# Four VectorE sums at a kernel's end made two, and the stores of banks 5 and 7 joined

## The chip, the core and the metric

The kernel runs on one core of a Trainium2 chip. The metric is device time in microseconds (us), the median of several executions. Time before: 98.53 us, the median of three runs (97.7 to 98.61).

## What is computed

The input x is 8 images of 64 channels and 32 x 32 pixels, in float32. Two blocks follow one another. The first is a linear attention with 8 heads of 32 on the layer-normalised input, with its projection, bias and residual. The second is a 3 x 3 convolution of the sign of the input with the signs of the weights, then a batch norm over all images and pixels, and the residual. Only the second block's end matters here:

```python
def _L1_conv_ref(x, W, gamma, beta):
    s = jnp.sign(x)
    bw = jnp.sign(W)
    y = lax.conv_general_dilated(s, bw, window_strides=(1, 1), padding=((1, 1), (1, 1)), ...)
    mean = jnp.mean(y, axis=(0, 2, 3))
    var = jnp.var(y, axis=(0, 2, 3))
    inv = gamma / jnp.sqrt(var + BN_EPS)
    yn = (y - mean[None, :, None, None]) * inv[None, :, None, None] + beta[None, :, None, None]
    return yn + x
```

The output is 8 x 64 x 32 x 32 in float32, 2 MB in all.

## The kernel before, in words

Two images lie side by side on the 128 partitions: image 2q on partitions 0 to 63 and image 2q+1 on 64 to 127, for the four pairs q. An image has 1024 pixels, two halves of 512. The instructions of each engine are written out by hand in one list per engine, and semaphores order the engines among one another: `t_ready` counts what ScalarE has scaled, `o_ready` what VectorE has summed, `x1_moved` the transfers that bring parts of x into place, `stored` and `stored_pool` the stores.

The convolution leaves its 8 x 512 columns in the eight banks of PSUM (`ps`), one bank per 128 x 512 block. Banks 0 and 1 hold the two halves of images 0 and 1 (pair 0) with the images on their usual partitions. Banks 2 and 3 hold pair 1 with the partitions of the two images exchanged, so image 3 is on partitions 0 to 63 and image 2 on 64 to 127. Bank 4 has the first half of pair 2 and bank 6 that of pair 3, straight; banks 5 and 7 hold the second halves of these pairs, exchanged. The residual x must match: for banks 0, 1, 4 and 6 it is read from `X`, for 2, 3, 5 and 7 from `X1`, which SyncE's transfers of L282 and L286 fill with the partitions exchanged.

TensorE's last convolutions are those of pairs 2 and 3 (L1002). Then a short serial part makes the batch norm's scale and shift (`bn`), of columns of one element (L710 to L775). After it comes the end of the kernel, which the change touches. It works in nine pieces in the order of `FINALS` (L46): bank 4 in two halves of 256 columns, then banks 6, 0, 1, 5, 7, 2, 3.

- ScalarE (L559) writes scale x y of one piece into `OUT`, one ACTIVATE per piece. Bank 0 it reads from `Y`, a float16 copy of that bank in SBUF.
- VectorE (L781) adds shift and residual to it in place, one SCALAR_TENSOR_TENSOR per piece.
- SyncE stores. It issues a store of 128 KB for each half of bank 4, one of 256 KB for bank 6 (L291), one of 512 KB for banks 0 and 1 together after the sum of bank 1 (L293), then the stores of partitions 0 to 63 of banks 5, 7 (L296), 2 and 3 (L299), 128 KB each.
- GpSimd (POOL) issues the stores of partitions 64 to 127 of banks 5, 7 (L391), 2 and 3 (L394), 128 KB each. Its descriptors are made in software; the profile has these stores on the queue q0, and SyncE's on q1.

SyncE's last wait is for all twelve stores (8 and 4). ScalarE's order of pieces is not touched by the change.

```python
for i, piece in enumerate(FINALS):
    dve.wait_ge(t_ready, i + 1)
    wait_residual(dve, piece)
    nc.vector.scalar_tensor_tensor(cut(OUT, piece), cut(OUT, piece), bn[:, BN_SHIFT], residual(piece),
                                   op0=ALU.add, op1=ALU.add).then_inc(o_ready, 1)
```

Of the kernel before, what the change touches and what calls it, by code (L numbers as in the profile page):

```python
# [5 lines left out]
def attention_then_binary_conv(nc, x, ln_g, ln_b, w_qkv, w_out, b_out, conv_w, bn_gamma, bn_beta, out):  # L6
# [11 lines left out]
    B, C, H, W = x.shape  # L18
    P = 128
    N = H * W  # L20
# [5 lines left out]
    PAIRS = B // 2  # L26
    BANK = 512
# [15 lines left out]

    HALF = BANK // 2
    PIECES = {"4a": (4, 0, HALF), "4b": (4, HALF, BANK), **{str(j): (j, 0, BANK) for j in range(8)}}
    FINALS = ("4a", "4b", "6", "0", "1", "5", "7", "2", "3")  # L46
    ACT_STATS = (2, 3)
    RECORDS = 4
# [3 lines left out]
    out_d = out.rearrange("b c h w -> b c (h w)")  # L52
# [4 lines left out]
    with ExitStack() as ctx:  # L57
        def sb(name, shape, dt=f32):
            return ctx.enter_context(nc.sbuf_tensor(name, shape, dt))

        def sem(name):
            return ctx.enter_context(nc.semaphore(name))
# [34 lines left out]
        X = sb("X", [P, PAIRS, N])  # L97
# [23 lines left out]
        X1 = sb("X1", [P, B, BANK])  # L121
        OUT = sb("OUT", [P, B, BANK])
# [5 lines left out]
        bn = sb("bn", [P, 5])  # L128
        BN_SPREAD, BN_LN, BN_INV, BN_SCALE, BN_SHIFT = (slice(i, i + 1) for i in range(5))
# [65 lines left out]
        t_ready, o_ready, stored, stored_pool = sem("t_ready"), sem("o_ready"), sem("stored"), sem("stored_pool")  # L195
# [5 lines left out]
                engine.wait_ge(hi_ready, n - 1)  # L201

        def wait_final(engine, piece):
            engine.wait_ge(o_ready, FINALS.index(piece) + 1)

        def cut(t, piece):
            j, first, end = PIECES[piece]
            return t[:, j, first:end]

        def residual(piece):  # L210
            j, first, end = PIECES[piece]
            if j < 2:
                return X[:, 0, j * BANK + first:j * BANK + end]
            return X[:, j // 2, first:end] if j in (4, 6) else X1[:, j, first:end]

        def wait_residual(engine, piece):
            j = PIECES[piece][0]
            if j < 2 or j in (4, 6):
                engine.wait_ge(x1_ready, HALVES * (j // 2) + (2 if j < 2 else 1))
            else:  # L220
                engine.wait_ge(x1_moved[j // 2], 32)
# [20 lines left out]
        def _(sp):  # L242
# [15 lines left out]
            for h in range(HALVES):  # L258
                part = slice(h * BANK, (h + 1) * BANK)
# [28 lines left out]
            for piece in ("4a", "4b", "6"):  # L288
                j, first, end = PIECES[piece]
                wait_final(sp, piece)  # L290
                sp.dma_start(out_p[j // 2, :, first:end], OUT[:, j, first:end]).then_inc(stored, 16)  # L291
            wait_final(sp, "1")
            sp.dma_start(out_p[0], OUT[:, 0:2, :]).then_inc(stored, 16)  # L293
            for q in range(2, PAIRS):
                wait_final(sp, str(2 * q + 1))
                sp.dma_start(out_d[2 * q + 1, :, BANK:N], OUT[0:C, 2 * q + 1, :]).then_inc(stored, 16)  # L296
            for h in range(HALVES):
                wait_final(sp, str(2 + h))
                sp.dma_start(out_d[3, :, h * BANK:(h + 1) * BANK], OUT[0:C, 2 + h, :]).then_inc(stored, 16)  # L299
            sp.wait_ge(stored, 16 * 8)  # L300
            sp.wait_ge(stored_pool, 16 * 4)

        @block.gpsimd
        def _(pool):
# [81 lines left out]
                    nc.gpsimd.tensor_tensor(e_lo, e, e_hi, ALU.subtract).then_inc(elo_pool, 1)  # L386

            nc.gpsimd.memset(act_records[:, :, 0:1], float(len(ACT_STATS) * BANK // RECORDS)).then_inc(st_counts, 1)
            for q in range(2, PAIRS):
                wait_final(pool, str(2 * q + 1))  # L390
                pool.dma_start(out_d[2 * q, :, BANK:N], OUT[C:P, 2 * q + 1, :]).then_inc(stored_pool, 16)  # L391
            for h in range(HALVES):
                wait_final(pool, str(2 + h))
                pool.dma_start(out_d[2, :, h * BANK:(h + 1) * BANK], OUT[C:P, 2 + h, :]).then_inc(stored_pool, 16)  # L394
# [2 lines left out]
        def _(act):  # L397
# [159 lines left out]
            act.wait_ge(scale_ready, 1)  # L557
            for piece in FINALS:
                nc.scalar.activation(cut(OUT, piece), cut(ps, piece) if piece != "0" else Y[:], ACT.Identity,  # L559
# [3 lines left out]
        def _(dve):  # L563
# [211 lines left out]
            nc.vector.scalar_tensor_tensor(bn[:, BN_SHIFT], fs_ps[:, 0:1], bn[:, BN_SCALE], vec[:, OUT_:OUT_ + 1],  # L775
                                           op0=ALU.mult, op1=ALU.add).then_inc(affine_ready, 1)
            dve.wait_ge(affine_ready, 1)
            for i, piece in enumerate(FINALS):
                dve.wait_ge(t_ready, i + 1)
                wait_residual(dve, piece)  # L780
                nc.vector.scalar_tensor_tensor(cut(OUT, piece), cut(OUT, piece), bn[:, BN_SHIFT], residual(piece),  # L781
                                               op0=ALU.add, op1=ALU.add).then_inc(o_ready, 1)

        @block.tensor
# [407 lines left out]
```

## Time and profile before

| | |
|---|---|
| median of three runs | 98.53 us |
| the profiled execution | 98.15 us |
| its span in the trace | 96.4 us |
| TensorE (PE) busy in the span | 80.3 us |
| VectorE (DVE) busy | 62.0 us |
| ScalarE (ACT) busy | 57.0 us |
| GpSimd (POOL) busy | 43.6 us |
| bytes written to HBM | 2.10 MB |

The profile describes one execution. Its own time is 1.75 us longer than the span, which runs from the first to the last recorded event. Positions in the trace are us from the span's start. Busy shares over the whole span say little about the end of the kernel, where TensorE has nothing left to do, so this document reads the last ten microseconds by themselves.

### The profile page before, as it was taken

To read this page: it belongs to the slowest core of one execution; us is meant where nothing else is said; L and a number is where in the kernel's file an instruction comes from. 1 tells how busy PE (TensorE), PEld (TensorE's weight loads), DVE (VectorE), ACT (ScalarE), POOL (GpSimd) and SP (SyncE) were. 2 spreads that over 40 slices of the span, in tenths; PEclk is the share of its full clock that TensorE was granted. 3 is DMA by queue.
4 is the path that set the end of the run, shared out by engine and by line. 5 is a ranking of instruction groups with operands and counts; after the bars stand their busy time and mean duration, and the time that the engine had idled before them with its cause. 6 is when DMAs were issued, how large, how long until landed. Compare 5 with 4: busy or idle time off the path is not lost.

```text
span 96.4 us, 2071 instructions
## 1 busy us (share of the span) xinstructions
PE 80.3 (83%) x763; PEld 46.4 (48%) x763; DVE 62.0 (64%) x125; ACT 57.0 (59%) x113; POOL 43.6 (45%) x58
## 2 busy tenths in 40 slices
PE   4999988999999899999999999999999999410000
PEld 4624433357576357565756747767664544210000
DVE  5723587985499708836965499719935359639920
ACT  5024967788799559079492753777601479069700
POOL 6912789469671594162495093586400000000440
PEclk9999999999999999999999999999999999995555
DMA  2799013314300123000033000001700404003795
GB/s 70 225 290 363 5 37 97 111 39 136 106 8 0 51 63 107 7 0 0 0 108 113 0 0 0 0 7 24 194 7 0 109 7 100 9 0 127 298 259 190
DMA packets 4613, 7.87 MB, mean 82 GB/s; under 512 B 1410, under 2 KB 1982, under 8 KB 4604
## 3 DMA queue, kind: packets, MB, share of 16 engines
q1 hardware_dynamic: 4140, 7.16, 23.5%
q0 software_dynamic: 192, 0.52, 1.8%
q8 instruction: 6, 0.10, 0.5%
q10 hardware_dynamic: 272, 0.07, 0.3%
q14 instruction: 3, 0.02, 0.1%
HBM read 2.51 MB, written 2.10 MB: 48 GB/s over the span
## 4 chain that ended last, share of the span: by engine, by line
PE 71%; DVE 13%; ACT 6%; issue 4%; POOL 2%; POOLq 1%; DVEq 0%
PE ps L899 9%; PE ps L913 8%; PE ps L900 7%; PE ps L990 5%; PE ps L1002 4%; PE ps L925 4%; PE ps L793 4%; PE ps L970 4%; PE ps L862 4%; DVE mx L629 4%; PE ps L945 3%; DVE OUT L781 2%; PE ps L952 2%; PE ps L931 2%; PE ps L1042 2%
## 5 line engine op out<-in xcount | busy, mean ns | idle before, releaser
L634 DVE TENSOR_REDUCE mxp<-ps 128x2 bf16<-128x1024 f32 x12 | 14.7, 1223 | 10.9 <-PE ps L862 10.8
L476 ACT ACTIVATE E<-ps 128x512 f32<-128x512 f32 x32 | 17.8, 596 | 3.4 <-PE ps L900 3.2
L386 POOL TENSOR_TENSOR E_lo<-E 128x512 bf16<-128x512 f32 x11 | 12.5, 1161 | 7.1 <-ACT E L476 7.1
L899 PE MATMUL ps<-wk_max,S 128*128 128x256 bf16 x64 | 15.2, 275 | 0.0
L900 PE MATMUL ps<-wk_lo,S 128*128 128x256 bf16 x64 | 15.1, 272 | 0.0
L391 POOL DMA_DIRECT2D out<-OUT x2 | 1.2, 605 | 22.0 <-DVE OUT L781 22.0
L405 ACT ACTIVATE sq<-ps 128x512 f32<-128x512 f32 x8 | 4.8, 601 | 8.3 <-DVE bn_eps L599 3.7
L342 POOL TENSOR_TENSOR x_lo<-XN,x_hi 128x512 bf16<-128x512 f32 x8 | 9.2, 1156 | 0.9 <-DVE x_hi L610 0.8
L702 DVE SCALAR_TENSOR_TENSOR X<-XN,vec,ps 128x1024 f32<-128x1024 f32 (+1 forms) x5 | 5.2, 1066 | 5.4 <-PE ps L970 5.4
L899 PEld LDWEIGHTS ps<-wk_max,S 128*128 128x128 bf16 x64 | 6.2, 97 | 4.3 <-issue 1.5
L331 POOL CAST x_hi<-XN 128x512 bf16<-128x512 f32 x6 | 3.7, 611 | 9.4 <-DVE XN L604 9.4
L913 PE MATMUL ps<-E,XT 128*64 128x256 f32 x64 | 7.8, 385 | 0.0
L483 ACT COPY PT<-ps 128x256 f32<-128x256 f32 x8 | 3.0, 372 | 7.5 <-PE ps L931 5.6
L409 ACT ACTIVATE lnv<-ps,eps 128x512 f32<-128x512 f32 x8 | 5.5, 683 | 2.7 <-PE ps L814 2.7
L900 PEld LDWEIGHTS ps<-wk_lo,S 128*128 128x128 bf16 x64 | 6.3, 98 | 1.2 <-issue 0.3
L604 DVE TENSOR_TENSOR XN<-ps,rstd 128x512 f32<-128x512 f32 x8 | 5.5, 685 | 1.9 <-ACT rstd L415 1.7
L316 POOL TENSOR_TENSOR x_rest<-X 128x512 f32<-128x512 f32 x4 | 4.2, 1040 | 3.9 <-DMA X<-in_x 3.9
L487 ACT ACTIVATE SG<-X,vec 128x1024 bf16<-128x1024 f32 (+1 forms) x5 | 4.8, 980 | 1.9 <-DVE X L702 1.9
L781 DVE SCALAR_TENSOR_TENSOR OUT<-OUT,bn,X 128x512 f32<-128x512 f32 (+1 forms) x9 | 5.6, 689 | 0.3 <-ACT OUT L559 0.3
L793 PE MATMUL ps<-X,center_mat 128*128 128x512 f32 x8 | 5.7, 856 | 0.1
L629 DVE TENSOR_REDUCE mx<-ps 128x1 bf16<-128x1024 f32 x4 | 4.9, 1223 | 1.2 <-PE ps L851 1.1
L913 PEld LDWEIGHTS ps<-E,XT 128*64 128x64 f32 x64 | 4.2, 136 | 2.5 <-issue 0.7
(148 smaller groups left out, 167.0 us busy)
## 6 DMA issues: line engine op xcount, KB each, us to landing
X<-in_x SPq DMA_DIRECT2D x3, 512.0 KB, 4.5
S<-x_hi SPq DMA_DIRECT2D x7, 126.0 KB
S<-x_lo SPq DMA_DIRECT2D x7, 126.0 KB
out<-OUT SPq DMA_DIRECT2D x6, 128.0 KB, 2.9
X<-in_x SPq DMA_DIRECT2D x2, 256.0 KB, 3.0
X<-X SPq DMA_DIRECT2D x2, 256.0 KB, 3.4
X<-X SPq DMA_DIRECT2D x4, 128.0 KB, 2.3
out<-OUT SPq DMA_DIRECT2D x1, 512.0 KB, 2.7
```

The source lines that it names most:

```text
L342: nc.gpsimd.tensor_tensor(x_lo[:, q, part], XN[:, q, part], x_hi[:, q, part], ALU.subtract).then_inc(lo_ready, 1)
L386: nc.gpsimd.tensor_tensor(e_lo, e, e_hi, ALU.subtract).then_inc(elo_pool, 1)
L409: nc.scalar.activation(lnv[:, n % 2, :], pv(n), ACT.Ln, bias=eps[:, 0:1]).then_inc(lnv_ready, 1)
L476: nc.scalar.activation(E[:, b % 2, 2 * g:2 * g + 2, :].rearrange("p k j -> p (k j)"), kt_ps[g % 2], ACT.Exp).then_inc(exp_ready, 1)
L604: nc.vector.tensor_tensor(XN[:, q, h * BANK:(h + 1) * BANK], pc(n), rstd[:, n % 2, :], ALU.mult).then_inc(scaled, 1)
L629: nc.vector.tensor_reduce(mx[:, d, t:t + 1], k_ps.rearrange("p a n -> p (a n)"), AX.X, ALU.max).then_inc(max_ready, 1)
L634: nc.vector.tensor_reduce(mxp[:, h, :, t], k_ps, AX.X, ALU.max).then_inc(max_ready, 1)
L781: nc.vector.scalar_tensor_tensor(cut(OUT, piece), cut(OUT, piece), bn[:, BN_SHIFT], residual(piece), op0=ALU.add, op1=ALU.add).then_inc(o_ ...
L793: nc.tensor.matmul(pc(n), center_mat[:], x_unit, start=True, stop=True).then_inc(centered, 1)
L899: nc.tensor.matmul(dst, chunk, wk_max[:, b % 2, :], start=True, stop=False)
L900: last = nc.tensor.matmul(dst, chunk, wk_lo[:], start=False, stop=True)
L913: last = nc.tensor.matmul(d_ps[d * C:d * C + C, :], XT[:, b, k, :], E[:, b % 2, k, :], start=(k < 2), stop=(k >= CH - 2))
```

## The change

VectorE makes seven sums instead of nine: the list `SUMS` says what each covers. The sum of bank 0 and that of bank 1 become one operation on 128 x 1024, and those of banks 5 and 7 one operation on 128 x 2 x 512 (banks 5 and 7 of `OUT` and `X1`, with bank 6 stepped over). Each waits until ScalarE has scaled its last member. ScalarE still scales bank by bank. SyncE's store of banks 0 and 1 waits for the merged sum, as one of 512 KB like before. SyncE's two stores of banks 5 and 7 become one of 256 KB, and so do GpSimd's two.

```diff
@@ -43,6 +43,7 @@
+    SUMS = ("4a", "4b", "6", "0+1", "5+7", "2", "3")
     FINALS = ("4a", "4b", "6", "0", "1", "5", "7", "2", "3")
@@ -201,7 +202,7 @@
         def wait_final(engine, piece):
-            engine.wait_ge(o_ready, FINALS.index(piece) + 1)
+            engine.wait_ge(o_ready, SUMS.index(piece) + 1)
@@ -289,16 +290,15 @@
-            wait_final(sp, "1")
+            wait_final(sp, "0+1")
             sp.dma_start(out_p[0], OUT[:, 0:2, :]).then_inc(stored, 16)
-            for q in range(2, PAIRS):
-                wait_final(sp, str(2 * q + 1))
-                sp.dma_start(out_d[2 * q + 1, :, BANK:N], OUT[0:C, 2 * q + 1, :]).then_inc(stored, 16)
+            wait_final(sp, "5+7")
+            sp.dma_start(out_d[5:8:2, :, BANK:N].rearrange("j c n -> c j n"), OUT[0:C, 5:8:2, :]).then_inc(stored, 16)
...
-            sp.wait_ge(stored, 16 * 8)
-            sp.wait_ge(stored_pool, 16 * 4)
+            sp.wait_ge(stored, 16 * 7)
+            sp.wait_ge(stored_pool, 16 * 3)
@@ -386,9 +386,9 @@
-            for q in range(2, PAIRS):
-                wait_final(pool, str(2 * q + 1))
-                pool.dma_start(out_d[2 * q, :, BANK:N], OUT[C:P, 2 * q + 1, :]).then_inc(stored_pool, 16)
+            wait_final(pool, "5+7")
+            pool.dma_start(out_d[4:8:2, :, BANK:N].rearrange("j c n -> c j n"), OUT[C:P, 5:8:2, :]
+                           ).then_inc(stored_pool, 16)
@@ -775,10 +775,19 @@
-            for i, piece in enumerate(FINALS):
-                dve.wait_ge(t_ready, i + 1)
-                wait_residual(dve, piece)
-                nc.vector.scalar_tensor_tensor(cut(OUT, piece), cut(OUT, piece), bn[:, BN_SHIFT], residual(piece),
+            for piece in SUMS:
+                members = piece.split("+")
+                dve.wait_ge(t_ready, FINALS.index(members[-1]) + 1)
+                for member in members:
+                    wait_residual(dve, member)
+                if piece == "0+1":
+                    part = OUT[:, 0:2, :].rearrange("p j n -> p (j n)")
+                    kept = X[:, 0, :]
+                elif piece == "5+7":
+                    part, kept = OUT[:, 5:8:2, :], X1[:, 5:8:2, :]
+                else:
+                    part, kept = cut(OUT, piece), residual(piece)
+                nc.vector.scalar_tensor_tensor(part, part, bn[:, BN_SHIFT], kept,
                                                op0=ALU.add, op1=ALU.add).then_inc(o_ready, 1)
```

VectorE's last instructions before, with the semaphores that each waits for (the first two rows are the halves of bank 4; the next covers banks 6, 0 and 1; then 5, 7, and 2 with 3):

```order
L781 SCALAR_TENSOR_TENSOR OUT<-OUT,bn,X 128x256 [waits x1_ready,t_ready,affine_ready]
L781 SCALAR_TENSOR_TENSOR OUT<-OUT,bn,X 128x256 [waits x1_ready,t_ready]
L781 SCALAR_TENSOR_TENSOR OUT<-OUT,bn,X 128x512 [waits x1_ready,t_ready] x3
L781 SCALAR_TENSOR_TENSOR OUT<-OUT,bn,X 128x512 [waits x1_moved2,t_ready]
L781 SCALAR_TENSOR_TENSOR OUT<-OUT,bn,X 128x512 [waits x1_moved3,t_ready]
L781 SCALAR_TENSOR_TENSOR OUT<-OUT,bn,X 128x512 [waits x1_moved1,t_ready] x2
```

And in the changed kernel:

```order
L790 SCALAR_TENSOR_TENSOR OUT<-OUT,bn,X 128x256 [waits x1_ready,t_ready,affine_ready]
L790 SCALAR_TENSOR_TENSOR OUT<-OUT,bn,X 128x256 [waits x1_ready,t_ready]
L790 SCALAR_TENSOR_TENSOR OUT<-OUT,bn,X 128x512 [waits x1_ready,t_ready]
L790 SCALAR_TENSOR_TENSOR OUT<-OUT,bn,X 128x1024 [waits x1_ready,t_ready]
L790 SCALAR_TENSOR_TENSOR OUT<-OUT,bn,X 128x2x512 [waits x1_moved3,x1_moved2,t_ready]
L790 SCALAR_TENSOR_TENSOR OUT<-OUT,bn,X 128x512 [waits x1_moved1,t_ready] x2
```

Banks 0 and 1 now stand in one row of 1024 columns, banks 5 and 7 in one of 2 x 512, which waits for the transfers of both pairs. Nothing else on VectorE has moved.

SyncE's last instructions before (L291 stores banks 4 and 6, L293 banks 0 and 1, L296 banks 5 and 7, L299 banks 2 and 3; L57 is the end of its list):

```order
L291 DMA out<-OUT 128x256 [waits o_ready] x2
L291 DMA out<-OUT 128x512 [waits o_ready]
L293 DMA out<-OUT 128x1024 [waits o_ready]
L296 DMA out<-OUT 64x512 [waits o_ready] x2
L299 DMA out<-OUT 64x512 [waits o_ready] x2
L57 UNCONDITIONAL_BRANCH [waits stored_pool,stored]
```

And in the changed kernel:

```order
L292 DMA out<-OUT 128x256 [waits o_ready] x2
L292 DMA out<-OUT 128x512 [waits o_ready]
L294 DMA out<-OUT 128x1024 [waits o_ready]
L296 DMA out<-OUT 64x2x512 [waits o_ready]
L299 DMA out<-OUT 64x512 [waits o_ready] x2
L58 UNCONDITIONAL_BRANCH [waits stored_pool,stored]
```

One store of 64 x 2 x 512 stands where two of 64 x 512 stood, and GpSimd's list changes in the same way.

## Rows read from the trace of the kernel before

**Rows 1.** Busy time by stretch; columns PE, PEld, DVE, ACT, POOL, clock, DMA share, GB/s

```profile
82.50:86.50 4.00, 0.90 (x8) 0.59 (x4) 2.05 (x5) 1.27 (x5) 0.00 (x0) 1.00 0.00 0
86.50:92.20 5.70, 0.00 (x0) 0.00 (x0) 5.61 (x9) 4.37 (x8) 1.64 (x3) 0.51 0.58 207
92.20:96.40 4.20, 0.00 (x0) 0.00 (x0) 0.00 (x0) 0.00 (x0) 0.60 (x2) 0.50 0.68 220
```

**Rows 2.** End of the chain that ended last: start us, us, what

```profile
89.40 0.76 DVE OUT L781
90.16 0.30 issue
90.45 1.21 POOL out L391 x2
...
92.55 0.54 POOLq L57
```

**Rows 3.** Timeline: pieces of ScalarE (banks 6, 1, 7, 3), VectorE (6, 0, 1, 3)

```profile
86.68 0.69 ACT L559 ACTIVATE OUT<-ps,bn 128x512 f32<-128x512 f32 x1
...
87.86 0.69 ACT L559 ACTIVATE OUT<-ps,bn 128x512 f32<-128x512 f32 x1
...
89.00 0.71 ACT L559 ACTIVATE OUT<-ps,bn 128x512 f32<-128x512 f32 x1
...
90.14 0.73 ACT L559 ACTIVATE OUT<-ps,bn 128x512 f32<-128x512 f32 x1
...
87.40 0.75 DVE L781 SCALAR_TENSOR_TENSOR OUT<-OUT,bn,X 128x512 f32<-128x512 f32 x1
...
88.07 0.75 DVE L781 SCALAR_TENSOR_TENSOR OUT<-OUT,bn,X 128x512 f32<-128x512 f32 x1
...
88.73 0.75 DVE L781 SCALAR_TENSOR_TENSOR OUT<-OUT,bn,X 128x512 f32<-128x512 f32 x1
...
91.39 0.75 DVE L781 SCALAR_TENSOR_TENSOR OUT<-OUT,bn,X 128x512 f32<-128x512 f32 x1
```

**Rows 4.** Groups by line, shapes apart: busy us, mean ns of one, idle us before

```profile
L781 DVE SCALAR_TENSOR_TENSOR OUT<-OUT,bn,X 128x512 f32<-128x512 f32 x7 | 4.7, 748 | 0.0
L702 DVE SCALAR_TENSOR_TENSOR X<-XN,vec,ps 128x1024 f32<-128x1024 f32 x3 | 3.8, 1280 | 4.0 <-PE ps L970 4.0
...
L702 DVE SCALAR_TENSOR_TENSOR X<-XN,vec,ps 128x512 f32<-128x512 f32 x2 | 1.4, 745 | 1.4 <-PE ps L970 1.4
```

**Rows 5.** Timeline: issues of stores by SyncE and GpSimd

```profile
89.51 0.33 SPq L293 DMA_DIRECT2D out<-OUT  x1
...
90.45 0.68 POOL L391 DMA_DIRECT2D out<-OUT  x1 [21.96 <-DVE OUT L781]
...
92.58 0.52 POOL L394 DMA_DIRECT2D out<-OUT  x1 [0.29 <-issue]
```

**Rows 6.** DMA queues, 91.5 to 92.0 and 92.0 to 92.5: packets, MB, share

```profile
q1 hardware_dynamic: 68, 0.12, 89.7%
...
q0 software_dynamic: 12, 0.05, 37.9%
```

**Rows 7.** Busy time by stretch of 0.5 us, columns as in rows 1

```profile
90.00:90.50 0.50, 0.00 (x0) 0.00 (x0) 0.50 (x2) 0.50 (x2) 0.05 (x1) 0.50 0.34 139
90.50:91.00 0.50, 0.00 (x0) 0.00 (x0) 0.50 (x2) 0.37 (x1) 0.50 (x1) 0.50 1.02 418
...
92.00:92.50 0.50, 0.00 (x0) 0.00 (x0) 0.13 (x1) 0.00 (x0) 0.28 (x1) 0.50 0.82 197
...
94.50:95.00 0.50, 0.00 (x0) 0.00 (x0) 0.00 (x0) 0.00 (x0) 0.00 (x0) 0.50 0.98 357
95.00:95.50 0.50, 0.00 (x0) 0.00 (x0) 0.00 (x0) 0.00 (x0) 0.00 (x0) 0.50 0.31 119
```

**Rows 8.** Stores of L291 (128 and 256 KB), then of L394 (128 KB)

```profile
DMA to landing us min/median/max: 1.9/1.9/2.0
...
DMA to landing us min/median/max: 3.3/3.4/3.5
```

## The prediction, made before the changed kernel ran

> **What bounds the kernel now.** I read four views in this order. First, the busy time of each engine by stretch [rows 1]: up to 86.5 us TensorE and the short serial batch-norm part set the pace, and the change touches nothing there. From 86.5 to 92.2 VectorE is busy for 5.61 of 5.70 us, and from 92.2 to the end of the span no compute engine works, while the DMA engines are at 68%. So the end has two halves: sums paced by VectorE, then stores that drain. Second, the chain that ended last [rows 2]: it runs through a sum of VectorE, then through GpSimd's store issues, the last near 92.6, and then to the end at 96.4. Third, the timeline of the pieces [rows 3] and of the store issues [rows 5]. Fourth, the DMA engines in steps of half a microsecond [rows 6, 7], because the chain doesn't say whether the last 3.8 us are the latency of one store or a backlog of several.
>
> They are a backlog. The first three stores (128, 128 and 256 KB) land 1.9 to 2.0 us after issue, with idle DMA engines before them, and GpSimd's last two, of 128 KB, take 3.3 to 3.5 us [rows 8]. That is 1.4 us of queueing. The DMA engines show it directly: from 90.5 to 95.0 the share is between 0.82 and 1.10 in each of the nine half microseconds (three of them stand in [rows 7]), and 0.31 in the last stretch with data. Data of the 512 KB store of banks 0 and 1 start to flow near 90.3 (a third of the full rate in the half microsecond from 90.0 [rows 7], 0.8 us behind the issue at 89.51 [rows 5]) and the last data at about 95.3 (a share of 0.31 in the stretch from 95.0). Thus 1.5 MB (banks 0, 1, 5, 7, 2, 3) flow in some 5 us, and after them about 1.1 us pass for completion. What sets the end is when this backlog starts, how fast it flows, and whether it runs dry.
>
> **VectorE, step by step.** Two sums of 512 columns follow each other at 88.73 - 88.07 = 0.66 us from start to start, although each lasts 0.75 [rows 3]: their ends overlap by 0.09. For 1024 columns the same operation takes 1.28 us [rows 4], on operands partly in PSUM; at 512 columns that form took 745 ns in this trace against 748 here, so I use 1.28 for both merged sums. With the same overlap the next sum starts 1.28 - 0.09 = 1.19 after it, against 2 x 0.66 = 1.33 for two. Each merge saves 0.14 us, both 0.28. I charge nothing for stepping over bank 6; bounds are zero and the cost of an unmerged pair, 0.14.
>
> Against that stands a wait. Before, the sum of bank 0 starts at 88.07. The merged one must wait for ScalarE's bank 1, which starts at 87.86 and lasts 0.69, so it ends at 88.55 [rows 3]. With 0.05 for the hand-over (bank 6 was scaled at 86.68 + 0.69 = 87.37 and its sum began at 87.40; bounds 0.02 and 0.10) the merged sum starts at 88.60: VectorE idles for 0.53 us, with all later sums queued behind it. It ends at 88.60 + 1.28 = 89.88, where the sum of bank 1 ended at 88.73 + 0.75 = 89.48. The sum of 5+7 can start at 88.60 + 1.19 = 89.79. ScalarE is ahead there: it scales bank 7 from 89.00 to 89.71 and the last piece from 90.14 to 90.87 [rows 3]. The wait for bank 7 is covered, by less than 0.1 us; if ScalarE is 0.1 later it costs up to that. The sum 5+7 ends at 89.79 + 1.28 = 91.07, bank 2 starts at 90.98 and bank 3 at 91.65, ending at 92.40, where it ended at 91.39 + 0.75 = 92.14 [rows 3]. The last sum is 0.53 - 0.28 = 0.26 us later.
>
> **The stores, step by step.** SyncE issues the store of 0+1 within 0.03 us of its sum, at 89.91 instead of 89.51: 0.40 later. The stores of bank 5 (sum from 89.40 to 90.15 before [rows 2]) are issued 0.92 later, those of bank 7 (90.81 before) 0.26 later, those of bank 2 and 3 also 0.26. So no store leaves earlier, and two instructions on SyncE and GpSimd are gone. Behind GpSimd's 5+7 stand its stores of 2 and 3, and only the end of the kernel waits for them.
>
> How far can the backlog absorb this? Its front moves from 90.3 to 90.7. The 512 KB at 418 GB/s [rows 7] last 1.25 us, to about 91.95. SyncE's 5+7 is issued at 91.10 and its data can flow 0.8 later, at 91.9: no gap. Then 256 KB more of it, 0.6 to 1.0 us by the 418 GB/s or the slower 250 seen when mostly SyncE's 2 KB rows of banks 5 and 7 flowed (0.12 MB in 91.5 to 92.0) [rows 6], so until 92.5 to 92.9. GpSimd's data come late: its first store was issued at 90.45 [rows 5] and q0 has no packet before the stretch from 92.0 [rows 6], 1.6 us later. With 0.30 for its hand-over [rows 2], the merged store is issued at 91.37 and flows from about 93.0. SyncE's bank 2 (issued 91.77, data from 92.6) fills the hole between. So I expect the DMA engines busy throughout, with a gap of at most 0.4 us.
>
> The backlog therefore ends later by about its later front, 0.40 us, less what fewer and larger stores give back, plus a gap if there is one. The bounds: it gives back at most the whole 1.4 us of queueing, less 0.26 of the later issue, so -1.1 us; it loses at most 0.40 for the front and 0.4 for a gap and some 0.35 for GpSimd (below), +1.15. I take +0.35, near the later front and a little under it, since the last issue is only 0.26 later.
>
> **GpSimd's merged issue** is a price that the trace doesn't show. For 64 x 512 it takes 0.52 to 0.68 us [rows 5]; for 64 x 2 x 512 it is between 0.52 and twice 0.6 = 1.2. At 0.6 it is done at 91.97, before bank 2 is summed (91.73 + 0.30 = 92.03), and costs nothing. At 1.2 it is done at 92.57, bank 2 goes out 92.57 to 93.09, and bank 3 at 93.1, instead of 92.58 before: 0.5 late, of which the queueing hides part. I take 0.9, halfway: done at 92.27, bank 2 until 92.79, bank 3 at 92.84, 0.26 late, which is the delay of VectorE anyway.
> The Trainium skill (DMA: Bandwidth & Descriptors, section Anatomy of one DMA) calls the generation of descriptors a small and variable part and says that many can be emitted before the extra cost shows. By that the merged issue would stay at about 0.6, the same sum as mine; no row before has a larger store of GpSimd to set beside it.
>
> The sum: 98.15 us of the profiled execution (span 96.4 and 1.75 around it) + 0.35 = 98.5. That execution lies 0.38 under the median of the three runs, 98.53; the middle of all four times is 98.34, so I forecast 98.34 + 0.35 = 98.7 us.
>
> **The rivals.**
> 1. The stores flow better. In the stretch from 92.0 the share is 0.82 and only 197 GB/s flow, and 357 GB/s in that from 94.5 [rows 7], so the engines seem held up while the 2 KB rows of 5 and 7 from both queues mix. If the merged stores, which overlap less, flow like the late stretch, the 0.22 MB between 91.5 and 92.5 need 0.63 instead of 1.0 us and those to 93.5 likewise about 0.2 less. That gives 0.55 back against 0.40: -0.15, 98.2 us. For it speaks the uneven rate; against it, that the same rows, the same 64 partitions and the same two queues remain.
> In the Trainium skill (DMA: Bandwidth & Descriptors, section Bandwidth) the rule is to batch transfers, towards 1 MiB, and the section on one DMA gives each a fixed 2.0 us. Its formula makes 2.3 us of a 128 KB store where the trace has 3.3 to 3.5, so by it 1.1 us are queueing; two stores fewer would be worth something only where their fixed parts lie one behind the other.
> Here a merged chain that removed all queueing of [rows 8] would give the -1.1 us above, 97.2 us. The issues stand 0.5 to 0.8 us apart while each store takes over 3, so the fixed parts overlap already; this has little chance.
> 2. VectorE alone decides and the stores follow the last issue: +0.26 and nothing more, 98.6 us. This differs from my forecast by the front of the backlog, and can hardly be told from it by time.
> 3. Slower by over 1%: the queue runs dry and GpSimd is late. The store of 5+7 leaves 0.92 us later than bank 5 did. If GpSimd's issue takes 1.2 us and its first data come later in proportion, near 93.6, the DMA engines drain SyncE's share by 93.0 and idle until then, and over 0.5 MB then flow behind it on q0. That is 0.40 of the front, 0.4 of a gap and 0.35 of GpSimd's last issue: +1.15, 99.5 us. It decides once the first packet of q0 comes after about 93.3. For it speaks the long 1.6 us from GpSimd's issue to data; against it, that 1.4 us of queueing are there to absorb a late last store.
> 4. The merged sums cost as much as two (1.5 us each), or the stepped one does: +0.14 to +0.28 on top of mine, 98.9 us. The row of 1.28 us for 1024 columns speaks against it.
>
> **How the numbers follow.** My case 0.47; rival 1 in its mild form 0.20, with a gain of over 1 us 0.03; rival 2 0.13; rival 3 0.10; rival 4 0.07. About 1% is what a measurement of this kernel can tell from no change, near 1 us. Forecast, rivals 1 (mild), 2 and 4 lie within it, though their upper tails reach over; so faster 0.06, same 0.82, slower 0.12. The range goes from 97.9, below the mild rival 1 by a spread like that of the runs (0.3), to 99.5, the whole of rival 3: it leaves out the large gain and the outer spread of either side.
>
> **What would show each step.** The merged sum of 0 and 1 starts near 88.6 after an idle time of about 0.5 us that ScalarE ended, and lasts 1.28; the last sum starts near 91.65. The issue of the 512 KB store stands at 89.9, the last issue of GpSimd near 92.8. The DMA share stays near 1 from 90.8 to 95.3 and data end near 95.7. I would be wrong if the DMA engines run empty between 92 and 93.5 (rival 3), if the last stores land in less than 3 us although they are issued later (rival 1), or if GpSimd's merged issue takes over 1.1 us.

## The result, and the profile after

The changed kernel takes 99.09 us in the median (98.84 to 99.69, 4 runs), the kernel before 98.12 us in the same comparison (97.11 to 98.61, 4 runs). The ratio is 1.0138, with a 95% interval of 1.0088 to 1.0189: the change makes the kernel 1.4% slower. The ratio leaves out runs over 1.5% above the fastest of their kernel, here the one of 98.61 us, and so is larger than the quotient of the medians (1.0099). The forecast was 98.7 us. The range of 97.9 to 99.5 holds the result, but the likeliest case was "within 1%", and the measured ratio lies above that. What holds it is the upper end, which came from rival 3 and not from the case that was forecast.

The profiled execution took 99.19 us, with a span of 97.4 us against 96.4. Its busy time by stretch answers to the last two of [rows 1]. Columns are PE, PEld, DVE, ACT, POOL, granted clock, DMA share, GB/s:

```profile
86.50:92.20 5.70, 0.00 (x0) 0.00 (x0) 5.19 (x7) 4.11 (x8) 1.08 (x2) 0.50 0.48 184
92.20:97.40 5.20, 0.00 (x0) 0.00 (x0) 0.00 (x0) 0.00 (x0) 0.72 (x2) 0.50 0.78 203
```

VectorE works less (5.19 for 5.61 us), the DMA engines carry less beside it (share 0.48 for 0.58), and the stretch in which no compute engine works is 5.2 us instead of 4.2. The loss shows there.

One more thing is needed to set traces side by side. Everything up to the first piece that ScalarE scales is untouched, yet it begins at other times in other executions: at 85.95 us in the kernel before, at 85.69 here, between 85.0 and 86.5 in the runs below. So I call **the tail** the time from that start to the end of the span: 96.4 - 85.95 = 10.45 us before, 97.4 - 85.69 = 11.71 after. The tail is 1.26 us longer. Where the two are compared, 0.26 is to be added to a time of after. Every tail is that of one execution, with the span read to 0.1 us.

The timeline of the pieces and of the store issues answers to [rows 3, 5]:

```profile
87.61 0.69 ACT L559 ACTIVATE OUT<-ps,bn 128x512 f32<-128x512 f32 x1
...
88.33 1.28 DVE L790 SCALAR_TENSOR_TENSOR OUT<-OUT,bn,X 128x1024 f32<-128x1024 f32 x1 [0.44 <-ACT OUT L559]
...
89.64 0.33 SPq L294 DMA_DIRECT2D out<-OUT  x1
89.53 1.28 DVE L790 SCALAR_TENSOR_TENSOR OUT<-OUT,bn,X 128x1024 f32<-128x1024 f32 x1
...
90.84 0.71 SPq L296 DMA_DIRECT2D out<-OUT  x1
91.12 0.76 POOL L390 DMA_DIRECT2D out<-OUT  x1 [22.89 <-DVE OUT L790]
...
91.39 0.75 DVE L790 SCALAR_TENSOR_TENSOR OUT<-OUT,bn,X 128x512 f32<-128x512 f32 x1
...
92.24 1.82 SPq L299 DMA_DIRECT2D out<-OUT  x1
92.43 0.52 POOL L394 DMA_DIRECT2D out<-OUT  x1
```

VectorE does what was worked out, nearly to the hundredth. The sum of banks 0 and 1 waits 0.44 us for ScalarE and starts 88.33 - 85.69 = 2.64 us after the scaling began (forecast 88.60 - 85.95 = 2.65). The store of banks 0 and 1 goes out after 3.95 us (forecast 3.96). The last sum ends at 92.14, after 6.45 us (forecast 6.45; 6.19 before). So VectorE's part, 0.40 us at the front and 0.26 at the last sum, is as forecast, and the rest of the loss is elsewhere.

The DMA engines in half microseconds answer to [rows 7]:

```profile
91.00:91.50 0.50, 0.00 (x0) 0.00 (x0) 0.50 (x2) 0.00 (x0) 0.38 (x1) 0.50 0.95 393
91.50:92.00 0.50, 0.00 (x0) 0.00 (x0) 0.50 (x1) 0.00 (x0) 0.50 (x2) 0.50 0.51 205
92.00:92.50 0.50, 0.00 (x0) 0.00 (x0) 0.14 (x1) 0.00 (x0) 0.47 (x2) 0.50 0.54 123
92.50:93.00 0.50, 0.00 (x0) 0.00 (x0) 0.00 (x0) 0.00 (x0) 0.46 (x1) 0.50 0.94 197
93.00:93.50 0.50, 0.00 (x0) 0.00 (x0) 0.00 (x0) 0.00 (x0) 0.00 (x0) 0.50 0.97 172
...
95.50:96.00 0.50, 0.00 (x0) 0.00 (x0) 0.00 (x0) 0.00 (x0) 0.00 (x0) 0.50 0.93 201
96.00:96.50 0.50, 0.00 (x0) 0.00 (x0) 0.00 (x0) 0.00 (x0) 0.00 (x0) 0.50 0.67 238
```

Two things are new. From 91.5 to 92.5 the engines are half idle (0.51 and 0.54). And from 92.5 to 93.5 they are busy to 94% and 97%, but move only 172 to 197 GB/s, where they moved 393 from 91.0. The DMA queues of 93.0 to 93.5 and of 93.5 to 94.0 say whose data these are:

```profile
q1 hardware_dynamic: 42, 0.09, 97.2%
...
q0 software_dynamic: 32, 0.13, 88.2%
q1 hardware_dynamic: 24, 0.02, 19.1%
```

Until 93.5 SyncE's queue q1 is alone, with its store of 64 partitions. GpSimd's first packet starts at 93.56, 2.44 us behind the issue at 91.12; before it started at 92.19, 1.74 us behind the issue at 90.45 [rows 5]. The last stores pay for it. L299 (SyncE, banks 2 and 3) landed after 3.3 to 3.4 us before (the first line here), L394 (GpSimd) after 3.3 to 3.5 [rows 8]. The second line is L299 in the changed kernel, the third L394:

```profile
DMA to landing us min/median/max: 3.3/3.4/3.4
...
DMA to landing us min/median/max: 4.1/4.4/4.8
...
DMA to landing us min/median/max: 4.2/4.3/4.3
```

The last to land is SyncE's store of bank 3: issued at 92.24, plus 4.8, is 97.0. SyncE's issue of it lasts 1.82 us, where the corresponding one of before lasted 0.73. That long issue is over at 94.06, while the store of bank 2, ahead of it on q1, ends only between 94.6 and 95.3. So nothing here shows that the issue itself held the last data back.

### The profile page after: what moved, and what is told of

It is laid out like the page before. It is cut to its first block, busy times and chain, and to the rows that moved or that the text cites. A ratio compares the mean times of both kernels' runs of the same rounds, so it can differ in the third digit from the quotient of the medians.

```text
span 97.4 us, 2065 instructions
## 1 busy us (share of the span) xinstructions
PE 79.4 (82%) x763; PEld 46.2 (47%) x763; DVE 62.4 (64%) x123; ACT 57.0 (59%) x113; POOL 43.3 (44%) x57
## 4 chain that ended last, share of the span: by engine, by line
PE 67%; DVE 13%; ACT 6%; issue 3%; DMA 3%; POOL 2%; ACTq 0%; DVEq 0%
PE ps L908 8%; PE ps L922 8%; PE ps L909 7%; PE ps L999 5%; PE ps L1011 4%; PE ps L934 4%; PE ps L979 4%; PE ps L871 4%; DVE mx L629 4%; PE ps L802 3%; PE ps L954 3%; DMA X<-in_x 3%; DVE XN L604 2%; PE ps L961 2%; ACT OUT L559 2%
## 5 line engine op out<-in xcount | busy, mean ns | idle before, releaser
L790 DVE SCALAR_TENSOR_TENSOR OUT<-OUT,bn,X 128x512 f32<-128x512 f32 (+2 forms) x7 | 5.4, 824 | 0.8 <-ACT OUT L559 0.8
L802 PE MATMUL ps<-X,center_mat 128*128 128x512 f32 x8 | 5.1, 772 | 0.3 <-DMA X<-in_x 0.3
```

The lines of the kernel that those rows point to most:

```text
L790: nc.vector.scalar_tensor_tensor(part, part, bn[:, BN_SHIFT], kept, op0=ALU.add, op1=ALU.add).then_inc(o_ready, 1)
L802: nc.tensor.matmul(pc(n), center_mat[:], x_unit, start=True, stop=True).then_inc(centered, 1)
```

## The experiments

Each run is compared with the kernel before on the same chip. "Tail" is the time from the first scaled piece to the end of the span in the one profiled execution of each kernel.

| run | what is joined or changed | ratio to before | 95% interval | tail, us |
|---|---|---|---|---|
| before | nothing | | | 10.45 |
| the change | both sums, stores of 5 and 7 | 1.0138 | 1.0088 to 1.0189 | 11.71 |
| e1 | sum of 0 and 1 alone | 1.0066 | 1.0023 to 1.0109 | 10.92 |
| e2 | sum of 5 and 7, and their stores | 1.0145 | 1.0070 to 1.0220 | 11.66 |
| e3 | the stores alone | 1.0108 | 1.0063 to 1.0152 | 11.49 |
| e4 | both sums alone | 1.0116 | 1.0054 to 1.0178 | 11.44 |
| e5 | nothing; bank 5's stores wait for bank 7 | 1.0094 | 1.0058 to 1.0130 | 11.11 |
| e6 | SyncE's store alone | 1.0055 | 1.0015 to 1.0096 | 10.80 |
| e7 | GpSimd's store alone | 1.0034 | 0.9995 to 1.0072 | 10.80 |
| e8 | as e3, each store over 128 partitions | 1.0032 | 0.9997 to 1.0068 | 10.75 |
| e9 | as e3, other places in HBM | 1.0104 | 1.0055 to 1.0153 | 11.40 |
| p2 | as before, upper halves issued by ScalarE | 1.0032 | 0.9988 to 1.0077 | 10.32 |
| p3b | as before, two of them by ScalarE | 0.9979 | 0.9935 to 1.0022 | 10.39 |
| p4 | as before, half stores first | 1.0083 | 1.0043 to 1.0124 | 10.77 |

**e1: the sum of banks 0 and 1 alone.**

```diff
-    SUMS = ("4a", "4b", "6", "0+1", "5+7", "2", "3")
+    SUMS = ("4a", "4b", "6", "0+1", "5", "7", "2", "3")
```

with the stores of 5 and 7 apart as before. What was expected: 

> Only the sums of banks 0 and 1 are merged; 5 and 7 are summed and stored one by one as before. Theory M (the joined stores of banks 5 and 7 cost the most: a store over 64 partitions alone on the DMA engines moves some 190 GB/s, and GpSimd's data come late): +0.2 to +0.4 us against before, from VectorE's wait for bank 1, without an empty stretch of the DMA engines after 91.7 us and without a stretch of over 1 us in which q1 alone is busy. Rival W (VectorE's wait for bank 1, which delays every later store, is what costs): nearly the whole loss, +1.0 us or more.

Measured: +0.66%, about 0.65 us, and a tail longer by 0.47 us. The interval begins at +0.23%, so the loss is real and its size less sure. It is somewhat more than theory M's 0.2 to 0.4, far less than W's 1.0, and the tail fits the step of the prediction that put the front of the backlog 0.40 us later. The trace has none of the half-empty stretches (columns as above):

```profile
91.50:92.00 0.50, 0.00 (x0) 0.00 (x0) 0.50 (x1) 0.00 (x0) 0.40 (x2) 0.50 0.89 254
92.00:92.50 0.50, 0.00 (x0) 0.00 (x0) 0.15 (x1) 0.00 (x0) 0.31 (x1) 0.50 0.92 201
```

**e2: banks 5 and 7 alone**, sum and stores:

```diff
-    SUMS = ("4a", "4b", "6", "0+1", "5+7", "2", "3")
+    SUMS = ("4a", "4b", "6", "0", "1", "5+7", "2", "3")
```

What was expected: 

> Banks 0 and 1 are summed apart as before; 5 and 7 are summed in one and stored together. M: most of the loss, +0.8 to +1.2 us. VectorE waits about 0.3 us for ScalarE's bank 7 and its last sum ends some 0.2 us later. W: +0.2 us at most, since no wait for bank 1 is left.

Measured: +1.45%, a tail longer by 1.21 us. Without any wait for bank 1, the whole loss of the change is there. W is out as the main cause. VectorE is not quite as before, though: the merged sum waits 0.27 us for ScalarE's bank 7, and the last sum ends 0.21 us later (6.40 us after the first scaled piece, for 6.19). e3 takes that away.

**e3: the stores alone.** The nine sums are as before, `SUMS` is equal to `FINALS`, and both joined stores wait for the sum of bank 7:

```diff
-            wait_final(sp, "5+7")
+            wait_final(sp, "7")
```

What was expected: 

> VectorE's nine sums as before; only the stores of banks 5 and 7 are joined, both issued after the sum of bank 7. M: +0.6 to +1.0 us although no sum is late. W: 0 within 0.2 us.

Measured: +1.08%, a tail longer by 1.04 us, although no sum has moved and nothing was taken from or added to VectorE. Two DMA issues fewer, and a microsecond lost.

**e4: the sums alone**, both merged, and the stores of 5 and 7 apart but both behind the merged sum:

```diff
-            sp.dma_start(out_d[5:8:2, :, BANK:N].rearrange("j c n -> c j n"), OUT[0:C, 5:8:2, :]).then_inc(stored, 16)
+            for q in range(2, PAIRS):
+                wait_final(sp, "5+7")
+                sp.dma_start(out_d[2 * q + 1, :, BANK:N], OUT[0:C, 2 * q + 1, :]).then_inc(stored, 16)
```

What was expected: 

> Both pairs of sums are merged as in the change, but banks 5 and 7 are stored by two stores on either queue, issued one after the other behind the merged sum. M in the form that the joined transfer itself is slow: +0.3 to +0.5 us. M in the form that only the late start of bank 5's store counts (no half-finished data to overlap with banks 0 and 1): about the same as the change, +1.0 us or more. W: as the change too.

Measured: +1.16%, a tail longer by 0.99 us. So a loss of this size does not need a joined transfer, as the form with the late start had it. The merged sum of 0 and 1 is in this run too, and it alone makes the tail 0.47 us longer (e1), so e4 doesn't show that a late bank 5 is enough. e5 tests that.

**e5: the late start by itself.** Nine sums, four stores for banks 5 and 7, and only the wait of bank 5's stores changed to the sum of bank 7:

```diff
-                wait_final(sp, str(2 * q + 1))
+                wait_final(sp, "7")
```

and the same on GpSimd. What was expected: 

> Nine sums as before, and banks 5 and 7 stored apart as before, but the stores of bank 5 wait for the sum of bank 7 too. Theory L (the loss is the late start: data of bank 5 no longer follow banks 0 and 1 without a hole): +0.7 to +1.1 us against before, as with the joined stores alone (+1.08%). Theory J (joining makes the transfers slow, because q1's 256 KB run before anything of q0 and in one piece): +0.3 us or less, and packets of q1 near 84 ns once q0 is active.

Measured: +0.94%, a tail longer by 0.66 us. Theory L holds by the ratio, and the interval leaves out the 0.3 us of J: stores of bank 5 that wait 0.66 us longer, and whose bytes were not the last to leave, cost 0.9 us (0.66 by the tail). The gap of the DMA engines (share 0.48) and the slow stretch after it (189 GB/s) are both there, in the stretches from 92.0 and 92.5:

```profile
92.00:92.50 0.50, 0.00 (x0) 0.00 (x0) 0.37 (x1) 0.00 (x0) 0.50 (x2) 0.50 0.48 115
92.50:93.00 0.50, 0.00 (x0) 0.00 (x0) 0.00 (x0) 0.00 (x0) 0.50 (x2) 0.50 0.89 189
```

Whether joining adds something of its own is not settled. The tails say 0.38 us (1.04 against 0.66), the ratios 0.14% with intervals far wider than that. The packets give a reason for a difference of that kind: q1 flows alone from 92.16 to 93.52 in e3, 1.36 us, and from 92.25 to 92.88 in e5, 0.63 us.

**e6 and e7: one queue at a time.** Nine sums; in e6 only SyncE's store of 5 and 7 is joined, in e7 only GpSimd's. What was expected of e6: 

> Nine sums, only SyncE's stores of 5 and 7 are joined; GpSimd stores 5 and 7 one by one as early as before. L: about half of the loss, +0.3 to +0.6 us, the hole after 91.7 us is partly filled by q0 from 92.0. J with q1 at fault: +0.7 to +1.0 us.

And of e7: 

> Nine sums, only GpSimd's stores of 5 and 7 are joined; SyncE's are as before. The first packet of q0 moves from 92.1 to some 93.4 us. L: no hole after 91.7, q1 alone runs at about 200 GB/s until then: +0.4 to +0.7 us. J with q0 at fault: +0.8 us or more; J with q1 at fault: within 0.3 us of before.

Measured: +0.55% and +0.34%, with equal tails of 10.80 us (+0.35). The two together (e3) lose 1.08%. While one queue's bank 5 is on time its data fill the hole, so each alone costs about half of L's sum or less. For e7 that is under the 0.4 to 0.7 us that L had forecast, and near what J gave it with q1 at fault; e5 is what speaks against J. The stretch from 91.0 in e6 has GpSimd's data alone, in e7 SyncE's alone, one row of each:

```profile
91.00:91.50 0.50, 0.00 (x0) 0.00 (x0) 0.28 (x1) 0.00 (x0) 0.43 (x1) 0.50 1.13 238
...
91.00:91.50 0.50, 0.00 (x0) 0.00 (x0) 0.18 (x1) 0.00 (x0) 0.47 (x2) 0.50 0.81 209
```

Either queue alone with a store of 64 partitions moves 209 to 238 GB/s, GpSimd's over partitions 64 to 127, SyncE's over 0 to 63. That led to the question of the next two runs: why are these transfers slow?

**When GpSimd's data start.** e3 and e7 have the same joined store on GpSimd, and it is issued 5.16 us after the first scaled piece in both (91.07 - 85.91 and 90.16 - 85.00). Only SyncE's stores differ. In e3 q0's first packet starts at 93.52, 2.45 us behind the issue; in e7 at 91.80, 1.64 us behind it. So the larger store of GpSimd is not what makes its data late. The packets' own times in the traces say what goes with it: q0 starts when the SyncE store that was issued before it is ending. A store ends with 16 short packets. Those of that SyncE store start from 92.17 to 92.36 in the kernel before, and q0 at 92.19; from 93.55 to 93.80 in the changed one, and q0 at 93.56; from 91.85 to 92.02 in e8 below, and q0 at 92.05. In all thirteen kernels of this document in which GpSimd stores, q0's first packet lies between the start of the first of these packets and 0.04 us behind the end of the last. Two consecutive stretches of e8, from 91.5 and from 92.0, have q1 alone and then q0 alone:

```profile
q1 hardware_dynamic: 85, 0.14, 76.9%
...
q0 software_dynamic: 43, 0.18, 95.4%
q1 hardware_dynamic: 1, 0.00, 0.1%
```

**e8: the same stores over all partitions.** As e3, but SyncE stores bank 5 whole and GpSimd bank 7 whole. The exchange of the two images in the second halves of pairs 2 and 3 is left out.

```diff
-            sp.dma_start(out_d[5:8:2, :, BANK:N].rearrange("j c n -> c j n"), OUT[0:C, 5:8:2, :]).then_inc(stored, 16)
+            sp.dma_start(out_p[2, :, BANK:N], OUT[:, 5, :]).then_inc(stored, 16)
```

What was expected: 

> Nine sums and joined stores in number, bytes, row length and time of issue (after the sum of bank 7), but SyncE stores bank 5 over all 128 partitions and GpSimd bank 7 likewise. It leaves out the exchange of the two images of pairs 2 and 3 in their second halves. Theory P (a store over 64 partitions uses only half of SBUF's side, some 200 GB/s while it is alone): packets of 2 KB on q1 fall from 145 to 189 ns to near 84 ns, q1 alone moves over 350 GB/s, and the time falls by 0.5 us or more under the kernel with joined stores (+1.08%), to within 0.4 us of before. Rival H (the rows' places in HBM make them slow): packets stay over 140 ns and the time at +0.9 us or more.

Measured: +0.32% with an interval that reaches below zero, a tail of 10.75 us instead of 11.49. The intervals of e3 and e8 overlap only from 0.63% to 0.68%. The bytes, the row length, the number of stores and the point of issue are those of e3, and 0.7 us are back. The queue q1 of e8 from 91.5 to 92.0, with rows of 2 KB over 128 partitions, has the first line above; for e3 here is the same queue from 92.5 to 93.0, over 64:

```profile
q1 hardware_dynamic: 47, 0.10, 92.3%
```

The share is of 16 engines over 0.5 us, which is 8 us of engine time. In e3 0.923 x 8 = 7.4 us over 47 packets is 157 ns for a packet of 2 KB. In e8 0.769 x 8 = 6.15 us over 85 packets is 72 ns; 15 of these are the short ones that end a transfer, so it is near 88 ns for one of 2 KB. Over the whole half microsecond q1 moved 287 GB/s, not the 350 that P expected, since the engines were busy for 77% only. The rival H is not yet out by this, since e8 also changes which images the queues write.

The time that is back is not that of the rate alone. SyncE's issue of the store is shorter too, first e3, then e8:

```profile
90.79 0.71 SPq L296 DMA_DIRECT2D out<-OUT  x1
...
90.33 0.33 SPq L296 DMA_DIRECT2D out<-OUT  x1
```

Its data start 1.37 us behind the issue in e3 (at 92.16) and 0.84 us behind it in e8 (at 91.17). So the DMA engines are empty from 91.73 to 92.16 in e3 and not at all there in e8. e8 shows what half-partition stores cost here in rate and start together. It also bounds theory L: with bank 5 as late as in e5, but over all partitions, the tail is only 0.30 us longer.

**e9: the same partitions, other places.** As e3, but the joined stores fill the whole 4 KB rows of images 3 and 2, and those of banks 2 and 3 go where 5 and 7 belonged. The results stand in the wrong images, and that is all that is changed.

```diff
-            sp.dma_start(out_d[5:8:2, :, BANK:N].rearrange("j c n -> c j n"), OUT[0:C, 5:8:2, :]).then_inc(stored, 16)
+            sp.dma_start(out_d[3].rearrange("c (j n) -> c j n", j=2), OUT[0:C, 5:8:2, :]).then_inc(stored, 16)
```

What was expected: 

> Nine sums, joined stores, issued as in the run with joined stores alone and from the same 64 partitions of the same banks; only the places in HBM differ: the two joined stores go to the whole 4 KB rows of images 3 and 2, and the four stores of banks 2 and 3 to the second halves of images 5, 4, 7 and 6. It leaves the results in the wrong images. Theory P (reading 64 partitions is what is slow): packets of 2 KB on q1 stay at 140 ns or more while q1 runs alone, and the time stays within 0.3 us of the run with joined stores alone (+1.08%). Rival H (rows of 2 KB at a stride of 4 KB, or these images' places, are slow): packets near 84 ns and at least 0.4 us less.

Measured: +1.04%, a tail of 11.40 us, as e3 (its profiled execution, 99.69 us, was the longest of its six). Its q1 alone is as slow as before. Here are the queue from 93.0 to 93.5 (0.958 x 8 / 48 = 160 ns a packet) and two stretches:

```profile
q1 hardware_dynamic: 48, 0.10, 95.8%
```

```profile
93.00:93.50 0.50, 0.00 (x0) 0.00 (x0) 0.00 (x0) 0.00 (x0) 0.49 (x1) 0.50 0.96 197
93.50:94.00 0.50, 0.00 (x0) 0.00 (x0) 0.00 (x0) 0.00 (x0) 0.00 (x0) 0.50 0.95 164
```

The slow rate follows the 64 source partitions, not the place in HBM. For the rate, theory P is shown by the pair e8 and e9; what inside the chip makes it so, no run here shows.

**p2 and p3b: halves side by side in the kernel before.** In p2 ScalarE issues all four stores of partitions 64 to 127, after its last piece; in p3b only those of banks 2 and 3.

```diff
+            for q in range(2, PAIRS):
+                wait_final(act, str(2 * q + 1))
+                act.dma_start(out_d[2 * q, :, BANK:N], OUT[C:P, 2 * q + 1, :]).then_inc(stored_pool, 16)
```

and likewise for banks 2 and 3, with GpSimd's taken out. What was expected of p2: 

> The kernel before, with the four upper-half stores (banks 5, 7, 2, 3, partitions 64 to 127) issued by ScalarE after its last piece instead of by GpSimd. If the two halves must flow side by side to use the DMA engines (theory P), data of the upper halves should begin some 0.8 us after issue instead of 1.6, and both halves share the engines in packets of one kind: 0.3 to 0.8 us faster than before. If the stores' total is limited by HBM or by the issue of the last one (rival H), within 0.2 us of before; if ScalarE's four issues of 0.5 us each come too late (the last near 92.9 against 92.6), up to 0.3 us slower.

And of p3b: 

> The kernel before, with the upper halves of banks 2 and 3 issued by ScalarE; GpSimd still issues those of 5 and 7. P: up to 0.4 us faster than before, less if q0 has its backlog from banks 5 and 7 anyway. Rival H: within 0.2 us of before, like the run with all four on ScalarE.

Measured: +0.32% (-0.12% to +0.77%) and -0.21% (-0.65% to +0.22%). Neither is told from no change; the gain of 0.3 us or more that I expected of p2 did not come. The trace of p2 does show the halves sharing the engines well, with 340 and 336 GB/s from 91.5 to 92.5:

```profile
91.00:91.50 0.50, 0.00 (x0) 0.00 (x0) 0.35 (x1) 0.00 (x0) 0.00 (x0) 0.50 1.01 197
91.50:92.00 0.50, 0.00 (x0) 0.00 (x0) 0.00 (x0) 0.00 (x0) 0.00 (x0) 0.50 0.94 340
92.00:92.50 0.50, 0.00 (x0) 0.00 (x0) 0.00 (x0) 0.00 (x0) 0.00 (x0) 0.50 1.04 336
```

The pieces start 0.77 us earlier in this execution (85.18 for 85.95), so the same microsecond of the kernel before is 92.27 to 93.27, with 229 and 283 GB/s:

```profile
92.27:92.77 0.50, 0.00 (x0) 0.00 (x0) 0.00 (x0) 0.00 (x0) 0.21 (x2) 0.50 0.92 229
92.77:93.27 0.50, 0.00 (x0) 0.00 (x0) 0.00 (x0) 0.00 (x0) 0.33 (x1) 0.50 0.95 283
```

Until 91.5 SyncE's half is alone again, at 197 GB/s. ScalarE's first store was issued at 89.40 and its first packet starts at 91.52, 2.1 us later and not the 0.8 us that I expected. By then SyncE's store of bank 5 is ending, as with q0 above. So the halves share the engines only after that, and the time during which one flows alone is not saved. The tail is 0.13 us shorter than before, less than a comparison of this kernel resolves.

**p4: half stores first.** The kernel before with its pieces in another order, so that the last stores run over all partitions:

```diff
-    FINALS = ("4a", "4b", "6", "0", "1", "5", "7", "2", "3")
+    FINALS = ("4a", "4b", "5", "7", "2", "3", "6", "0", "1")
```

with banks 0 and 1 stored apart. What was expected: 

> The kernel before with another order of pieces: bank 4, then 5, 7, 2, 3, then 6, 0, 1. The stores over 64 partitions start early, beside the sums, and the last two stores are SyncE's over all 128 partitions, 256 KB each (banks 0 and 1 apart). Theory P: the slow stores over one half are covered by the sums and the last ones land about 2 us after issue instead of 3.4: 0.5 to 1.2 us faster than before. Rival H (the total of bytes after the sums decides, whatever the partitions): within 0.3 us of before.

Measured: +0.83%, a tail longer by 0.32 us. A miss of both theories in size, and of P in sign. The stretches from 88.5 to 90.0 and the one from 94.0:

```profile
88.50:89.00 0.50, 0.00 (x0) 0.00 (x0) 0.50 (x2) 0.50 (x2) 0.50 (x2) 0.50 0.11 35
89.00:89.50 0.50, 0.00 (x0) 0.00 (x0) 0.50 (x2) 0.50 (x2) 0.45 (x1) 0.50 0.75 168
89.50:90.00 0.50, 0.00 (x0) 0.00 (x0) 0.50 (x2) 0.50 (x2) 0.45 (x1) 0.50 0.78 176
...
94.00:94.50 0.50, 0.00 (x0) 0.00 (x0) 0.00 (x0) 0.00 (x0) 0.00 (x0) 0.50 1.05 406
```

The slow halves now run beside the sums, as intended, but the DMA engines are first nearly empty and then at 168 to 176 GB/s just when they could work ahead. By this reading of one trace the backlog is larger afterwards, and 406 GB/s at the end don't make up for it: it is moved, not covered. No run tests that reading.

No run beats the kernel before by more than its interval.

## Where the prediction was right and where it was wrong, step by step

The time lies in the range and moved the way that was forecast. The mechanism of the forecast is not what happened: 0.35 us were forecast, the tail grew by 1.26.

**Right: VectorE.** The wait for bank 1, 1.28 us for a merged sum, no charge for stepping over bank 6, the start of every later sum and the issue at +0.40 us of the store of banks 0 and 1: all measured as worked out. The group of the two merged sums reads

```profile
L790 DVE SCALAR_TENSOR_TENSOR OUT<-OUT,bn,X 128x1024 f32<-128x1024 f32 x2 | 2.5, 1282 | 0.4 <-ACT OUT L559 0.4
```

against 1280 ns for the row that it was taken from [rows 4]. Rival 4 is out.

**Right: the later front of the backlog, as far as it goes.** The term of 0.40 us, by which I reached +0.35, is what e1 has by itself: a tail longer by 0.47.

**Nearly right: GpSimd's merged issue.** I took 0.9 us between bounds of 0.52 and 1.2; it is 0.76. By the Trainium skill (DMA: Bandwidth & Descriptors, section Anatomy of one DMA), which calls this part small, it would have stayed near 0.6. The trace has 0.76 for the joined store and 0.52 for each later one: less than two issues, more than one. It delayed little: GpSimd's last issue was at 92.43, which is 92.69 on the clock of before, against 92.58.

**Wrong: "So I expect the DMA engines busy throughout, with a gap of at most 0.4 us".** This is the step that failed, with three parts.

- The rate of the joined store was mis-sized. I gave SyncE's 256 KB "0.6 to 1.0 us"; from 92.21 to 93.80 it took 1.6 us, with 197 and 172 GB/s in the two full stretches of that time. The engines were busy in them, at half the rate. A sign of it was in the rows of before: the stretch from 92.0 had a share of 0.82 and 197 GB/s [rows 7]. I read it as two queues mixing. e8 and e9 show that 64 partitions alone give such a rate; how much of that one row is mixing stays open.
- The time until SyncE's data flow was carried over from the store of banks 0 and 1 over 128 partitions as 0.8 us. For the joined one over 64 partitions it was 1.37 (issue at 90.84, first packet at 92.21). The last packet of banks 0 and 1 ended at 91.90. So there was a hole of 0.3 us without any packet where "no gap" was expected; by the shares of 0.51 and 0.54 the engines were idle for about 0.5 us between 91.5 and 92.5.
- The time until GpSimd's data flow was carried over as 1.6 us; it was 2.4. So q0's first packet came at 93.56 (93.8 on the clock of before), and not near 93.0. By the pair e3 and e7 this goes with the joined store of SyncE ahead of it, which had to end first, and not with GpSimd's own store.

**Rival 3 came nearest, in price more than in mechanism.** It named a late store of 5 and 7 and late data of GpSimd, set the point of decision at a first packet of q0 after about 93.3, and priced it at +1.15 us, 99.5 us. The tail grew by 1.26 us. But it had GpSimd's issue at 1.2 us (0.76 measured) and idle engines in front of GpSimd's data. They were busy there, to 94% and 97%, at half the rate; the hole was in front of SyncE's store. That its price fits so well is in part luck. I gave it 0.10, and argued that 1.4 us of queueing would absorb a late store. That was the error of thought: the queueing absorbs lateness of the last store, while bytes that come late to a hole in the middle push everything behind them. e5 shows it by the wait of bank 5's stores alone. Rival 2 (+0.26, VectorE alone) is out by e3, in which no sum moves. Rival 1 is out too: its gain did not come, and a half that flows alone flows slower. The Trainium skill's rule to batch transfers (DMA: Bandwidth & Descriptors, section Bandwidth) gives no gain here: two transfers fewer went with +1.08% in e3.

**The parts do not add.** e1 (+0.66%) and e3 (+1.08%) make 1.74%, the change has 1.38%. e4, with late sums and late bank 5, has 1.16%. The intervals would allow a sum, but all of them draw on one backlog, so part of one delay may lie inside another.

## What to carry to other kernels

Where stores drain behind the last computation, look for the stretch in which the DMA engines could run dry or run slow, and ask what a merge does to the first bytes behind it; a merged operation releases its first part only when its last is done. Saved instructions are no gain by themselves: VectorE has two sums fewer here, its last sum still ends 0.26 us later, and the kernel lost 1.4%. A store that covers half of the partitions runs slowly while it is alone, so count it at its own rate. Whole-partition stores won 0.7 us of tail back in e8, against e3. Merely issuing the other half from a second queue (p2, p3b) or earlier (p4) made nothing faster here.

## What the runs showed of the hardware that I had not expected

- A transfer out of 64 partitions, alone on the DMA engines, moves 164 to 238 GB/s, while one out of 128 partitions with rows of the same 2 KB moves about twice that (406 GB/s in p4 from 94.0). The engines count as busy all the while: a packet of 2 KB takes 157 ns instead of 88. Busy share alone doesn't show it; share together with GB/s does.
- With the two halves on two hardware queues at once the total is 336 to 340 GB/s in the two stretches of p2 above.
- From an issue by GpSimd to its first data passed 1.7 us in the kernel before and 2.4 us in the changed one. In all these traces the first data come when the store issued before it by SyncE is ending; ScalarE's in p2 did the same, 2.1 us behind the issue.
- With the DMA engines empty, the first data of a SyncE store over 64 partitions came 1.2 us (e5) to 1.4 us (e3, the changed kernel) behind its issue; one over 128 partitions took 0.84 us in e8, where data of banks 0 and 1 were still flowing.
- The last issue on SyncE took 1.82 us behind a slow store, 0.73 before. In e8, where the store ahead was fast, no issue of SyncE's last two took over 0.53 us.
